# A graph network on one core: the table that TensorE reads for each batch of four products holds ten plain 16-bit words, not two packed ones

## What is computed

```python
h = _bn(x @ w1.T + b1, g1, beta1)
agg = jax.ops.segment_sum(h[src], dst, num_segments=n)
...
gathered = support[edge_col] * edge_val[:, None]
out = jax.ops.segment_sum(gathered, edge_row, num_segments=x.shape[0])
...
msg = h[src] * norm[:, None]          # three times, in the third layer
out = jax.ops.segment_sum(msg, dst, num_segments=n_nodes)
...
msg = jax.nn.relu(x[src] + edge_attr)
agg = jax.ops.segment_sum(msg, dst, num_segments=x.shape[0])
```

## Time and profile before

| | us |
|---|---|
| median of 3 runs (8908.18 to 8921.28) | 8915.93 |
| the profiled execution, its own time | 8895.57 |
| its span, first to last instruction | 8893.7 |
| POOL busy | 5629.0 (63%) |
| PE busy / PEld busy | 4488.3 (50%) / 2810.2 (32%) |
| DVE busy / ACT busy | 2097.8 (24%) / 478.7 (5%) |
| granted TensorE clock, mean | 0.696 |

### The profile page before, as it was taken

One profiled execution on the slowest core, in us unless ns is written; L12 is line 12 of the kernel. 1 busy time (PEld: TensorE's weight loads), 2 busy tenths in 40 slices (PEclk: granted clock), 3 DMA queues, 4 the chain that ended last, 5 costly groups with the idle time before them and its releaser, 6 DMA issues.

```text
span 8893.7 us, 66185 instructions
## 1 busy us (share of the span) xinstructions
PE 4488.3 (50%) x14394; PEld 2810.2 (32%) x14394; DVE 2097.8 (24%) x4052; ACT 478.7 (5%) x1352; POOL 5629.0 (63%) x5587
## 2 busy tenths in 40 slices
PE   3565441000684555535555645555555556455557
PEld 1333220000662333313333423322333334233335
DVE  5254100000151222231111201111211113344445
ACT  0000000000120000000000100000100001000002
POOL 5677777777106666646666366666366663677774
PEclk9676665555786666666767867677776768666668
DMA  2323311000012333333333233333233332566662
GB/s 78 91 83 89 93 38 35 1 1 1 3 43 88 91 92 92 91 92 91 92 92 92 80 93 91 91 91 89 88 92 92 92 91 61 171 181 182 181 181 69
DMA packets 423749, 774.80 MB, mean 87 GB/s; under 512 B 121790, under 2 KB 273268, under 8 KB 423412
## 3 DMA queue, kind: packets, MB, share of 16 engines
q0 software_dynamic: 250240, 616.54, 24.0%
q1 hardware_dynamic: 173172, 154.00, 5.5%
HBM read 730.40 MB, written 39.71 MB: 87 GB/s over the span
## 4 chain that ended last, share of the span: by engine, by line
PE 34%; issue 27%; another core or an unknown queue 21%; POOL 10%; DVE 5%; SPq 1%; DMA 1%; ACT 0%; ACTq 0%; DVEq 0%; POOLq 0%
PE acc L577 28%; POOL ring L426 10%; PE acc L494 2%; PE acc L489 2%; DVE onehot L1040 2%; DVE X L1069 1%; DMA ring<-table_x,idx_dst 1%; SPq L222 1%; PE bank L494 1%; SPq L198 0%; PE bank L489 0%; PE bank L480 0%; DVE stats L1066 0%; PE bank L498 0%
## 5 line engine op out<-in xcount | busy, mean ns | idle before, releaser
L577 PE MATMUL acc<-ring,onehot 128*128 x9984 | 3761.6, 517 | 3334.3 <-issue 2576.8
L577 PEld LDWEIGHTS acc<-ring,onehot 128*128 128x128 f32 x9984 | 2182.3, 247 | 4909.0 <-issue 4668.9
L426 POOL DMA_INDIRECT ring<-table_g,idx_dst x2346 | 2316.1, 987 | 1341.2 <-issue 684.4
L1040 DVE TENSOR_TENSOR onehot<-iota_row,dl_dst 128x512 f32<-128x512 f32 x1040 | 718.3, 693 | 4059.5 <-PE acc L577 2628.5
L426 POOL DMA_INDIRECT ring<-table_x,idx_dst x782 | 821.8, 1051 | 455.2 <-issue 359.2
L426 POOL DMA_INDIRECT ring<-in_x_dram,idx_dst x782 | 845.9, 1082 | 351.1 <-issue 245.6
L426 POOL DMA_INDIRECT ring<-table_y,E x782 | 743.0, 950 | 403.6 <-issue 227.6
L443 POOL DMA_INDIRECT records_by_src<-E x782 | 825.7, 1056 | 243.2 <-issue 243.2
L489 PE MATMUL acc<-H,wt_a 128*128 128x128 f32 x392 | 83.0, 380 | 712.1 <-issue 673.5
L1037 DVE TENSOR_SCALAR onehot<-iota_row,E 128x128 f32<-128x128 f32 x832 | 237.4, 358 | 845.2 <-PE acc L577 676.5
L1050 DVE TENSOR_TENSOR ring<-ring,E 128x1024 f32<-128x1024 f32 x196 | 239.8, 1224 | 497.5 <-DMA ring<-table_x,idx_dst 427.9
(11 more groups left out here) (278 smaller groups left out, 2184.4 us busy)
## 6 DMA issues: line engine op xcount, KB each, us to landing
E<-in_edge_attr_dram SPq DMA_DIRECT2D x781, 128.0 KB
ring<-table_g,idx_dst POOLq DMA_INDIRECT x2346
table_g<-H SPq DMA_DIRECT2D x147, 128.0 KB, 1.7
ring<-in_x_dram,idx_dst POOLq DMA_INDIRECT x782
records_by_src<-E POOLq DMA_INDIRECT x782
ring<-table_y,E POOLq DMA_INDIRECT x782
ring<-table_x,idx_dst POOLq DMA_INDIRECT x782
table_y<-ring SPq DMA_DIRECT2D x49, 128.0 KB, 1.7
```

The source lines that it names most:

```text
L426: pool.indirect_dma_start(out=ring_v[:, b % SLOTS, 0:D], out_offset=None, in_=table[name][:, :], in_offset=bass.IndirectOffsetOnAxis(ap=id ...
L577: pe.matmul(acc4[:, ds(to, width)], onehot[:, (q * BATCH + j) % ONEHOTS, :], ring[:, ds(slot, width)], start=False, stop=True, skip_group_ ...
L1040: last = tt(onehot[:, s:s + BATCH, :], iota_row[:, :].unsqueeze(1).to_broadcast((P, BATCH, P)), dl_ap[which][:, q * BATCH:(q + 1) * BATCH] ...
```

## The change

TensorE's table gets ten 16-bit words per batch: four ring offsets (slot times width), four PSUM offsets (bank times 512), the number of blocks and the number of banks to wait for. TensorE loads all ten into registers and uses them as they are; `field` and the shifts are gone. `pair_rows` on VectorE makes the ten words with eight instructions instead of fourteen. The `src` tables move from `E1` to a part of `H` that held the sorted records. `need` becomes 16-bit too, read by SyncE as before. The number of products, their order, the waits' values and the semaphores stay.

```diff
-        prow = {"dst": sb("prow_dst", [1, QB * 2], I32)}
-        need = {"dst": sb("need_dst", [1, 2 * P], I32)}
+        prow = {"dst": sb("prow_dst", [1, QB * WORDS], U16)}
+        need = {"dst": sb("need_dst", [1, 2 * P], U16)}
...
-            def field(word, j, bits):
-                up = word >> (j * bits) if j else word
-                return up if j == BATCH - 1 else up - (up >> bits) * (1 << bits)
...
-                    _, (slots, rest) = nc.values_load_multi_w_load_instructions(
-                        prow[which][0:1, 2 * q:2 * q + 2], engines=[ET.PE], min_val=0, max_val=(1 << 24) - 1,
...
+                    _, words = nc.values_load_multi_w_load_instructions(
+                        prow[which][0:1, WORDS * q:WORDS * (q + 1)], engines=[ET.PE], min_val=0, max_val=(SLOTS - 1) * W,
...
                     pe.wait_ge(sm("onehot_ready"), n * QB + q + 1)
-                    pe.wait_ge(sm(f"landed{n}"), rest & 1023)
-                    pe.wait_ge(sm(f"cleared{n}"), (rest >> 10) & 63)
-                    banks = rest >> 16
+                    pe.wait_ge(sm(f"landed{n}"), words[2 * BATCH])
+                    pe.wait_ge(sm(f"cleared{n}"), words[2 * BATCH + 1])
                     for j in range(BATCH):
-                        slot = nc.s_assert_within(field(slots, j, 6) * W, 0, (SLOTS - 1) * W,
+                        slot = nc.s_assert_within(words[j], 0, (SLOTS - 1) * W,
...
-                        to = nc.s_assert_within(field(banks, j, 2) * 512, 0, (BANKS - 1) * 512,
+                        to = nc.s_assert_within(words[BATCH + j], 0, (BANKS - 1) * 512,
...
-                to = prow[which][0:1, :].rearrange("p (q w) -> p q w", w=2)
-                part, last = (dl_ap[which][0:1, i * QB:(i + 1) * QB] for i in range(2))
-                link(stt(last, t[:, :, 3], 1024.0, b[:, :, 3], ALU.mult, ALU.add))
-                ts(last, last, 1025.0, None, ALU.add)
-                for word, number, size in ((0, "b", SLOTS), (1, "t", BANKS)):
+                to = prow[which][0:1, :].rearrange("p (q w) -> p q w", w=WORDS)
+                ts(to[:, :, 2 * BATCH], b[:, :, BATCH - 1], 1.0, None, ALU.add)
+                ts(to[:, :, 2 * BATCH + 1], t[:, :, BATCH - 1], 1.0, None, ALU.add)
+                for word, number, size, step in ((0, "b", SLOTS, W), (BATCH, "t", BANKS, 512)):
                     link(copy(low, s[number][0:1, :]))
                     link(ts(low, low, size - 1, None, ALU.bitwise_and))
-                    link(stt(part, low_v[:, :, 3], float(size), low_v[:, :, 2], ALU.mult, ALU.add))
-                    link(stt(part, part, float(size), low_v[:, :, 1], ALU.mult, ALU.add))
-                    link(stt(to[:, :, 0] if word == 0 else part, part, float(size), low_v[:, :, 0], ALU.mult, ALU.add))
-                link(stt(to[:, :, 1], part, 65536.0, last, ALU.mult, ALU.add))
+                    link(ts(to[:, :, word:word + BATCH], low_v, float(step), None, ALU.mult))
```

More of the change, by code:

```diff
@@ L11 @@
 I32 = mybir.dt.int32
+U16 = mybir.dt.uint16
 EPS = 1e-5
@@ L21 @@
 BANKS = 4
+WORDS = 10
 REC = 3
@@ L44, in gnn_kernel @@
     assert DH == 2 and HALF <= 512 and PAD > N and SLOTS >= T + 3 + 2 * BATCH
-    assert BATCH == 4 and BANKS == 4 and SLOTS == 64 and TT < 64 and B < 1024
+    assert WORDS == 2 * BATCH + 2 and SLOTS * W < 1 << 16 and B < 1 << 16 and SLOTS & (SLOTS - 1) == BANKS & (BANKS - 1) == 0
     rec_dram = nc.dram_tensor("records_by_src", (B * P, REC), F32).ap()
@@ L101, in gnn_kernel @@
         cols_i = sb("cols_i", [P, 2], I32)
-        E1 = sb("E1", [P, max(2 * PAIRS + B + 2 * QB + 2 * P, B * (REC + 1), EAS * D + B)])
+        E1 = sb("E1", [P, max(2 * PAIRS + B, B * (REC + 1), EAS * D + B)])
         rec_e = E1[:, 0:B * REC].rearrange("p (b w) -> p b w", w=REC)
@@ L109, in gnn_kernel @@
         pair_w = E1[:, B + PAIRS:B + 2 * PAIRS]
-        prow["src"] = E1[:, B + 2 * PAIRS:B + 2 * PAIRS + 2 * QB].bitcast(I32)
-        need["src"] = E1[0:1, B + 2 * PAIRS + 2 * QB:B + 2 * PAIRS + 2 * QB + 2 * P].bitcast(I32)
         EA = E1[:, 0:EAS * D].rearrange("p (s d) -> p s d", d=D)
@@ L140, in gnn_kernel @@
         rec_n = H[:, at:at + NAT * REC].rearrange("p (j e w) -> p j e w", j=KT, w=REC)
+        prow["src"] = H[0:1, at:at + QB * WORDS // 2].bitcast(U16)
+        need["src"] = H[0:1, at + QB * WORDS // 2:at + QB * WORDS // 2 + P].bitcast(U16)
+        assert QB * WORDS // 2 + P <= NAT * REC
         at += NAT * REC
@@ L564, in sum_pairs @@
                         between(q)
-                    _, (slots, rest) = nc.values_load_multi_w_load_instructions(
-                        prow[which][0:1, 2 * q:2 * q + 2], engines=[ET.PE], min_val=0, max_val=(1 << 24) - 1,
-                        skip_runtime_bounds_check_because="both words are packed from clamped fields of 24 bits")
+                    _, words = nc.values_load_multi_w_load_instructions(
+                        prow[which][0:1, WORDS * q:WORDS * (q + 1)], engines=[ET.PE], min_val=0, max_val=(SLOTS - 1) * W,
+                        skip_runtime_bounds_check_because="made of clamped numbers")
                     pe.wait_ge(sm("onehot_ready"), n * QB + q + 1)
-                    pe.wait_ge(sm(f"landed{n}"), rest & 1023)
-                    pe.wait_ge(sm(f"cleared{n}"), (rest >> 10) & 63)
-                    banks = rest >> 16
+                    pe.wait_ge(sm(f"landed{n}"), words[2 * BATCH])
+                    pe.wait_ge(sm(f"cleared{n}"), words[2 * BATCH + 1])
                     for j in range(BATCH):
-                        slot = nc.s_assert_within(field(slots, j, 6) * W, 0, (SLOTS - 1) * W,
+                        slot = nc.s_assert_within(words[j], 0, (SLOTS - 1) * W,
                                                   skip_runtime_bounds_check_because="a block's number modulo the ring")
-                        to = nc.s_assert_within(field(banks, j, 2) * 512, 0, (BANKS - 1) * 512,
+                        to = nc.s_assert_within(words[BATCH + j], 0, (BANKS - 1) * 512,
                                                 skip_runtime_bounds_check_because="a tile's number modulo the banks")
```

## The result

| | before | after |
|---|---|---|
| median of 5 runs, us | 8915.93 (8906.36 to 8921.28) | 8877.74 (8874.03 to 8890.08) |
| the profiled execution's span, us | 8893.7 | 8874.9 |
| POOL busy, us | 5629.0 | 5603.2 |
| granted TensorE clock, mean | 0.696 | 0.719 |

The ratio is 0.9966, with an interval of 0.9955 to 0.9976: the change is faster by 0.34%, some 30 us (the two medians alone lie 38 us apart). The prediction said faster by 68 us and the range held the time, but by the ratio the gain was less than half of it, and hardly any of it came from where the prediction had put it: of 128 us of waits 12 went. All times in this document are of executions that agree within 0.4% for one kernel on one chip; a single one, of the experiment pause_sparse, took 8348 us beside 7744 to 7758 and is left out of its ratio.

What follows compares the result with a forecast made beforehand. POOL was taken to wait for TensorE, slowed by an instruction budget while POOL gathers. Stalls -128 us and tails +60 us summed to -68 us, from a median of 8915.93 to 8848 us; range 8490 to 9070.

Steps and rivals of the forecast that it cites:

- 128 us of waits: POOL's waits for freed ring slots: stalls 20% rarer, -128 us of the 638 us open to the change.
- The load: TensorE's register load per batch: priced by the word at 268 ns, ten words 2.68 us, 2.14 us more than before.
- Rival B: TensorE's load of ten words costs hardly more than of two; sum -339 us, 8577 us; chance 0.14.
- The register work: TensorE's sequencer work per batch outside the load: falls from 2.46 to 1.1 us, making a fast batch 3.8 us.
- the ends of the sums: TensorE's work after POOL's last gather: 15 batches x 0.8 us x 5 sums, +60 us.
- The budget: While POOL gathers unbroken, TensorE gets 90 to 100 instructions of either kind through quickly, then crawls; 23 per batch replace 30.
- The slow batch of 9 in place of 11.25 us: TensorE's batch in the crawl: put at 9 us, giving a round of 27.9 us in place of 23.08 between POOL's stalls.
- Rival A: Only array instructions count, so stalls stay as frequent and each lengthens with the batch; +209 us, 9125 us; chance 0.31 including mixtures.
- Rival C: TensorE keeps up for good: all 638 us of stalls go and the tails shrink by 175 us, 8103 us; chance 0.05.
- The rest: Remaining effects counted at nothing, such as VectorE's `src` table some 3 us shorter but hidden beside TensorE's table matmuls.

Runs made afterwards that it cites:

- pause_sparse: Changed kernel with POOL pausing 2.88 us ahead of each 32nd gather in sums 2 to 4; 1.0180 of the kernel before, prompt chip.
- more_ops: Changed kernel with eight fused register instructions per batch in place of four, load unchanged; 1.0042 of the kernel before on a late chip, 0.9920 and 0.9933 on prompt ones.
- half_array: Changed kernel with TensorE reading 16-bit views, 8 array instructions per batch in place of 16, register instructions kept; 0.9852 of the kernel before, late chip.
- more_words: Changed kernel with fourteen words loaded per batch, four of them unused; 1.0055 of the kernel before, late chip.
- after_ts: Changed kernel with VectorE's one-hots made by tensor-scalar in place of tensor-tensor operations; 0.9985 of the kernel before on a late chip, 0.9877 on a prompt one.
- one_signal: Changed kernel with TensorE signalling once per batch in place of once per product; 0.9961 of the kernel before, late chip.

## Why the prediction was right or wrong

*The load.* 2.68 us were forecast, 2.387 measured. The words cost less than two words suggested: (3.322 - 2.387)/4 = 0.234 us a word, and some 0.05 to 0.07 us fixed. Rival B, a price that doesn't grow, is out for this table.

*The register work.* 1.1 us were forecast, 3.12 - 2.39 = 0.73 us measured; a plain offset costs 55 ns. A fast batch is 3.12 us and not 3.8, so the ends of the sums grew by 10 us together (0.3, 0.9, 2.1, 5.7 and 0.6) and not by 60.

*The budget.* This is the step that failed. From the earlier trace rows I took it that register and array instructions are worth the same to a limit. The changed kernel has 22 instructions in place of 30 (23 were forecast) and waits 716 us in place of 728; more_ops has 26 and waits no longer; half_array shows 1.40 us for each array instruction and nothing for the others. The -128 us were -12. The slow register instructions of the earlier trace rows I had read as the cause of the jam; without a single one of them the jam stayed as it was. The slow batch of 9 in place of 11.25 us, which carried the 20%, is 22.4 us in both kernels where the stretch is slow throughout. The earlier trace rows held the answer, array work alone in a 2.80 us step per pair of weight load and matmul, and the prediction quoted it.

*Rival A* had the right count, array instructions alone, but the wrong price: more_words shows that a stall doesn't lengthen with the batch. A POOL that waits for a late signal doesn't wait for a batch. Its grounds against itself, that 48 array instructions used up the budget in the earlier trace rows and 104 went through in the earlier trace rows, were not grounds for register instructions: what begins a slow stretch is open.

*Rival C* was right in a way that it could not know: on prompt chips TensorE keeps up for good. But there the kernel before does too.

*The rest.* Nothing was said on VectorE's one-hots against POOL's gathers, a term put at nothing without a reason. The page of before had them side by side, 950 ns a gather in sum 1 and 987 ns in sums 2 to 4, 37 ns x 2346 = 87 us, and the prediction used neither. On prompt chips this is all of the change's 58 to 65 us.

*On late chips*, where the prediction was made, the gain of 30 us is not explained to the end. In the traced pair the six sums' gathers are over 6.0, 4.2, 1.7, 4.3, 6.7 and 7.4 us sooner from their first, 30 us together, and the ends give back 10. POOL's busy time fell by 26 us, 17 of them in the gathers of the six sums, but after_ts shows that shorter gathers alone shorten no sum there. What does is open.

## What to carry to other kernels

A slow instruction in a trace need not be what holds up the others: look for who waits, and for how long after the work that it waits for was done, before pricing the instruction. When an edit on one engine shifts another's start, compare the mean durations of instructions that nobody touched; if one operation has 950 ns in one stage and 987 ns in another, find out what runs beside it first, since an operation with one input there gave more here (1.2%) than the change itself (0.8%). And a gain of under 1% should be measured on more than one chip: the same pair gave 0.9966 and 0.9921, and pauses of POOL that won 0.55% on one chip lost 2.9% on another, where they were half as long.

## What the runs showed of the hardware

- The same kernel takes 8.86 to 8.92 ms on some chips and 7.60 to 7.62 ms on others. On the former, while POOL issues its DMAs closely, there are stretches in which what TensorE has finished becomes known to other engines only at one array instruction per 1.40 us (28.0 us for 20, 22.4 us for 16, 11.2 us for 8). A quarter of the signals (one_signal) or 22 instructions a batch in place of 30 doesn't change that. TensorE goes on working meanwhile: at the end of such a stretch five signals came within 0.17 us. In the shorter slow stretches later in a sum a batch takes anything up to 18 us. What makes a chip one or the other, and what begins and ends a slow stretch, isn't known.
- A load of ten 32-bit words into TensorE's registers takes 1.08 or 2.40 us, alternating with an offset of 0 or 8 bytes in 16. Ten 16-bit words in steps of 20 bytes take 2.39 us at every offset, and a plain offset from a register costs one fused instruction of 55 ns for each product.
- A 128x512 tensor-tensor operation of VectorE lengthens an indirect DMA of POOL's only if it runs when that begins, by what is then left of it less 0.13 us: 0.95 us become up to 1.47. 128x128 tensor-scalar operations, some 800 in a sum, leave it at 950 ns.
